# VectorE's order within a state of a selective scan: two scans, multiply-add, two scans, multiply-add

## The chip, the cores and the metric

The kernel runs on one core of a Trainium2 chip (trn2), as one program. The metric is the device time of one execution in microseconds (us). Engines are named as in the profile: PE is TensorE (matmuls), PEld its weight loads, DVE is VectorE, ACT is ScalarE, POOL is GpSimd, SP is SyncE, which issues most of the DMAs.

## The reference, cut to what matters

The input x has 8 sequences of 512 tokens with 256 channels. An adaptive layer norm is followed by a selective state-space layer (512 inner channels, 16 states) and, after a second adaptive layer norm, by a mixture of 8 experts with the best two chosen for each token. The change lies in the state-space layer:

```python
dt = softplus(dt @ W_dt + b_dt)
dA = exp(dt[..., None] * A)                      # A = -exp(A_log), 16 states
dBu = (dt * xc)[..., None] * Bm[:, :, None, :]
h[t] = dA[t] * h[t-1] + dBu[t]                   # along the 512 tokens
y = einsum('blds,bls->bld', h, Cm) + D_skip * xc
y = y * silu(z)
```

Everything is float32.

## The kernel before

The program has four stages one after the other, with barriers between them. Stage A does the state-space layer and the routing scores, stage B sorts tokens to experts, stage C runs the experts, stage D puts the results together. Only stage A is touched.

In stage A the inner channels lie on the partitions, in 4 chunks of 128 (index `c`), and the 512 tokens along the row. A sequence is one call of `body(n, p, has_o, has_p, has_r)` on every engine. It loops over the 16 states `s`. Besides the states of sequence n, a body carries parts of the input side of sequence n+1 (`has_p`), loads and the first norm of n+2 (`has_r`), and the output side of n-1 (`has_o`), each written by hand behind a certain state. Bodies 1 to 5 have all three, body 0 has no `has_o`, body 6 no `has_r`, body 7 only `has_o`. Each engine works its own list strictly in the order of the code and waits on semaphores.

For one state s, in the order in which the data go:

- POOL multiplies `dBu = u * B` for each chunk (L450), into a ring of 8 buffers.
- ACT computes `dA = exp(dt * a)` for each chunk (`decays`, L597), into a ring of only 2 PSUM banks: the one for a scan may start when the scan two before it has ended.
- DVE scans each chunk along the tokens (`scan`, L975) into `hs`, of which there are two (by parity of the state).
- PE transposes the four 128-token tiles of the four chunks (`states(n, s, i)`, L771) into PSUM: tiles 0 and 1 into bank T0, tiles 2 and 3 into bank T1, in the order 0, 2, then 1, 3. Tile 0 waits until all four scans of the state are done and the last multiply-add has read T0. Tile 1 waits until the first multiply-add has read T0.
- DVE multiplies tiles 0 and 1 by C and adds them to y (`add_y(n, p, s, i)`, L986, and L983 for state 0).
- ACT multiplies tiles 2 and 3 by C (`times_c(n, p, s, k)`, L583), and PE adds them up in PSUM by transposing matmuls (`add_up`, L780). At the start of a body PE transposes the finished y of the sequence before (`y_t`, L789, which waits for its last multiply-add).

DVE runs one state ahead with its scans: in its pass s it scans state s+1 and does the multiply-adds of state s. ACT's matching list is: decays 0 and 1 of state s+1, `times_c(s, 0)`, decay 2, in some passes an extra of the first kind, decay 3, `times_c(s, 1)`, in some passes an extra of the second kind, and again decay 0 of the next state. In DVE's passes (numbered by DVE's s; ACT's own index is one higher) the extras of the first kind are the first norm of n+2 (`p_norm`, L503, pass 4), both silus with their table loads (L543, L547, pass 6), `o_norm` (L503, pass 7), the squares of n+2 (L517, pass 8), `scores_in` (L612, pass 9), softplus parts (L568 to L571, passes 10 and 11, L575, pass 12) and one z copy (L539, passes 13 and 14). Those of the second kind are the copies into the convolution (`conv_in`, L534, passes 2 to 5, in the list of the sequence before their taps on DVE, L956, which run at the end of passes 2 to 5), `o_xhat` (L503, pass 9), softplus parts (passes 10 and 11), z copies (passes 12 and 13) and `norm` (L523, pass 14). DVE's own extras all stand at the end of its pass, behind the last scan and multiply-add: `o_skip` in pass 0 (PE's first `add_up` of the sequence waits for it), statistics, the taps, residuals, the choice of experts, and `dt` and `u` of the next sequence.

Of the kernel before, what the change touches and what calls it, by code (L numbers as in the profile page):

```python
# [107 lines left out]
def stage_a(nc, ctx, sem, ident, oh, wts, T, dA, Q, MOD_PS, YT, mod_d, b_d, h_d, xhat_d, base_d, slotx_d,  # L108
            x, norm_w, W_in, conv_w, conv_b, W_x, W_dt, b_dt, A_log, D_skip, W_out, Wg, cT, wmod):
    with ExitStack() as own:  # L110
# [138 lines left out]
        def after(eng, s, value):  # L249

            if not (isinstance(value, int) and value <= 0):
                eng.wait_ge(s, value)
# [638 lines left out]
        def _(dve):  # L891
# [53 lines left out]
            def p_stats(n):  # L945
                dve.wait_ge(s_pload, 32 * (n + 1))
                after(dve, s_ln1r, n)
                stats("p", n, xin, 0, s_ln1)

            def conv(n, p, c, bank):  # L950
                dve.wait_ge(s_xi, n * CH + c + 1)
                for k in range(PAD):
                    late = PAD - k
                    if k > 0:
                        dve.wait_ge(s_tap, (n * CH + c) * PAD + k)
                    nc.vector.scalar_tensor_tensor(xc[:, p, c, late:], Q[:, bank, 0:L - late], cw[:, c, k:k + 1], xc[:, p, c, late:],  # L956
                                                   ALU.mult, ALU.add).then_inc(s_tap, 1)
# [9 lines left out]
            def scan(n, s, c):  # L967
                i = s * CH + c
                if c == 0 and s >= 2:
                    dve.wait_ge(s_tr, n * UNITS + TI * (s - 1))  # L970
                elif c == 0:
                    after(dve, s_tr, (n - 1) * UNITS + TI * (NS - 1 + s))
                dve.wait_ge(s_dA, n * UNITS + i + 1)
                dve.wait_ge(s_dBu, n * UNITS + i + 1)
                nc.vector.tensor_tensor_scan(hs[:, s % 2, c, :], dA[:, i % DA_RING, :], dBu[:, i % RING, :], 0.0,  # L975
                                             ALU.mult, ALU.add).then_inc(s_scan, 1)

            def add_y(n, p, s, i):
                dve.wait_ge(s_tr, n * UNITS + TI * s + 2 * i + 1)
                c_s = ct[:, p, i, s:s + 1]  # L980
                if s == 0:
                    after(dve, s_yT, n)
                    ins = nc.vector.tensor_scalar(y[:, i, :], T[:, 0, :], c_s, None, ALU.mult)  # L983
                else:
                    dve.wait_ge(s_y, DT * (n * NS + s - 1) + i + 1)
                    ins = nc.vector.scalar_tensor_tensor(y[:, i, :], T[:, 0, :], c_s, y[:, i, :], ALU.mult, ALU.add)  # L986
                ins.then_inc(s_y, 1)

            def o_skip(n, p):
                dve.wait_ge(s_yT, n + 1)  # L990
                dve.wait_ge(s_acc, 2 * NS * (n + 1))
                for c in range(CH):
                    def by_tile(v):
                        return v.rearrange("p (i t) -> p i t", i=TI)
                    nc.vector.scalar_tensor_tensor(by_tile(gT[:, c, :]), by_tile(xc[:, p, c, :]), dsk[:, c:c + 1],
                                                   YT[:, :, c * P:(c + 1) * P], ALU.mult, ALU.add).then_inc(s_g, 1)

            def o_resid_half(n, half):
                dve.wait_ge(s_op, TI * n + 2 * half + 2)
                if half == 0:  # L1000
                    after(dve, s_bast, 16 * n)
                at = slice(2 * half, 2 * half + 2)
                nc.vector.tensor_tensor(x1[:, at, :], modo[:, 0, :].unsqueeze(1).to_broadcast([P, 2, D]),
                                        Q[:, OB, :].rearrange("p (i d) -> p i d", d=D), ALU.mult).then_inc(s_opr, 1)

            def o_resid(n):
                dve.wait_ge(s_opr, 2 * n + 2)
                link(nc.vector.tensor_tensor(x1[:, :, :], x1[:, :, :], xres[:, :, :], ALU.add), "o", n)
                stats("o", n, x1, 1, s_x1)

            def o_stats(n):
                dve.wait_ge(s_xfm, n + 1)
                stats("o", n, xf, 2, s_xf)

            def o_scores(n):
                dve.wait_ge(s_scp, n + 1)
                nc.vector.tensor_copy(sc[:, :, :], Q[:, XB, 0:TI * E].rearrange("p (i e) -> p i e", i=TI)).then_inc(s_scr, 1)

            def o_top(n):
                dve.wait_ge(s_scr, n + 1)  # L1020
                carrier()
                for i in range(TI):
                    last = nc.vector.max(top[:, i, :], sc[:, i, :])
                link(last, "o", n)
                carrier()
                for i in range(TI):
                    last = nc.vector.max_index(tix[:, i, :], top[:, i, :], sc[:, i, :])
                nc.vector.tensor_tensor(vd[:, 0, :], top[:, :, 1], top[:, :, 0], ALU.subtract).then_inc(s_vd, 1)
                link(last, "o", n)
                link(nc.vector.tensor_copy(tif[:, :, :], tix[:, :, 0:2]), "o", n)  # L1030
                for k in range(2):
                    nc.vector.tensor_tensor(oh[:, k, bass.ds(n * TI, TI), :], iota8[:, :].unsqueeze(1).to_broadcast([P, TI, E]),
                                            tif[:, :, k].unsqueeze(2).to_broadcast([P, TI, E]), ALU.is_equal)

            def o_base(n):
                dve.wait_ge(s_ve, n + 1)
                w1, w2 = wts[:, 0, bass.ds(n * TI, TI)], wts[:, 1, bass.ds(n * TI, TI)]
                link(nc.vector.tensor_scalar(vd[:, 2, :], vd[:, 1, :], 1.0, None, ALU.add), "o", n)
                link(nc.vector.reciprocal(vd[:, 2, :], vd[:, 2, :]), "o", n)
                link(nc.vector.tensor_tensor(vd[:, 1, :], vd[:, 1, :], vd[:, 2, :], ALU.mult), "o", n)  # L1040
                nc.vector.tensor_copy(w1, vd[:, 2, :])
                nc.vector.tensor_copy(w2, vd[:, 1, :])
                link(nc.vector.tensor_tensor(vd[:, 3, :], vd[:, 1, :], vd[:, 2, :], ALU.add), "o", n)

                dve.wait_ge(s_xh, n + 1)
                for i in range(TI):
                    last = nc.vector.scalar_tensor_tensor(xf[:, i, :], xf[:, i, :], vd[:, 3, i:i + 1], modo[:, 3, :],
                                                          ALU.mult, ALU.mult)
                last.then_inc(s_scaled, 1)
# [10 lines left out]
            def body(n, p, has_o, has_p, has_r):  # L1060
                if not has_o:
                    for c in range(CH):
                        scan(n, 0, c)

                def next_scan(s, c):
                    if s + 1 < NS:
                        scan(n, s + 1, c)
                    elif has_p:
                        scan(n + 1, 0, c)

                for s in range(NS):
                    next_scan(s, 0)
                    add_y(n, p, s, 0)
                    next_scan(s, 1)
                    next_scan(s, 2)
                    add_y(n, p, s, 1)
                    next_scan(s, 3)
                    if has_o and s == 0:
                        o_skip(n - 1, 1 - p)
                    if has_r and s == 1:  # L1080
                        p_stats(n + 2)
                    if has_p and s in (2, 3, 4, 5):
                        conv(n + 1, 1 - p, s - 2, XB)
                    if has_o and s == 3:
                        o_resid_half(n - 1, 0)
                    if has_o and s == 5:
                        o_resid_half(n - 1, 1)
                        o_resid(n - 1)
                    if has_o and s == 8:
                        o_stats(n - 1)  # L1090
                    if has_o and s == 9:
                        o_scores(n - 1)
                    if has_o and s == 10:
                        o_top(n - 1)
                    if has_o and s == 11:
                        o_base(n - 1)
                    if has_p and s == 12:
                        dt_sum(n + 1, 1 - p)
                    if has_p and s == 13:
                        dt_x(n + 1, 1 - p)  # L1100
                counted(P_LINKS * has_r, O_LINKS * has_o)

            def epilogue():
# [11 lines left out]
                o_base(NB - 1)  # L1115

            sequences(dve, prologue, body, epilogue)


# [451 lines left out]
```

## Time and profile before

| | |
|---|---|
| median of 3 runs | 1910.93 us (1910.68 to 1912.01) |
| profiled execution | 1918.14 us, its span 1916.3 us |
| DVE busy | 1327.5 us, 69% of the span |
| PE busy | 1321.5 us, 69% |
| POOL busy | 973.6 us, 51% |
| ACT busy | 893.6 us, 47% |
| stage A | scans from 91.4 us to 1160.7 us |
| stage C | about 1340 to 1890 us |

An idle time in brackets behind a row is the time for which the engine stood still before that instruction, and the arrow names the engine, the tile and the line that ended it. In a timeline, instructions of one kind that follow each other on an engine are merged into one row (x2 is two of them).

### The profile page before, as it was taken

The page shows a single profiled execution, that of the slowest core. Times are in us where ns is not written, and L with a number is a line of the kernel's source. Part 1 is how long each engine was busy: PE and PEld are TensorE (multiplying, and loading weights), DVE is VectorE, ACT ScalarE, POOL GpSimd, SP SyncE. Part 2 cuts the span into 40 slices and gives each one's busy share as a digit, 9 for nine tenths or more (in the row PEclk, how much of TensorE's full clock was granted, in tenths as well). Part 3 has the DMA queues.
Part 4 walks back from the last instruction along what each step waited for, and adds up shares of the span by engine and source line. Part 5 has one row for each costly group of instructions (what it writes and reads, how often), then busy time and mean ns, then how long its engine had stood idle before and what let it go on. Part 6 is the DMA issues. An engine that isn't in the chain of part 4 may idle for free. (4 is left out here: it accounts for less than half of the span.)

```text
span 1916.3 us, 27619 instructions
## 1 busy us (share of the span) xinstructions
PE 1321.5 (69%) x7744; PEld 1067.5 (56%) x7745; DVE 1327.5 (69%) x2543; ACT 893.6 (47%) x1299; POOL 973.6 (51%) x920
## 2 busy tenths in 40 slices
PE   2566767666667666767766655103999999999970
PEld 0244555454555544545544544103899999999960
DVE  1397988989889989989989994312454545545538
ACT  2568667667567667577567562001222222222200
POOL 2287868767767866867767781472111111111110
PEclk7788888989788989888989887556999999999995
DMA  4611111212112213112112110796211111111218
GB/s 162 239 53 56 34 39 50 89 36 88 46 40 74 65 34 105 39 34 87 40 35 78 36 50 26 205 249 195 64 39 36 36 38 33 38 36 35 71 63 292
DMA packets 97672, 146.78 MB, mean 77 GB/s; under 512 B 10457, under 2 KB 66265, under 8 KB 97441
## 3 DMA queue, kind: packets, MB, share of 16 engines
q1 hardware_dynamic: 78112, 109.59, 18.3%
q10 hardware_dynamic: 12928, 18.14, 3.4%
q0 software_dynamic: 6528, 17.87, 3.0%
q8 instruction: 41, 0.67, 0.1%
q14 instruction: 63, 0.51, 0.1%
HBM read 101.14 MB, written 44.42 MB: 76 GB/s over the span
## 5 line engine op out<-in xcount | busy, mean ns | idle before, releaser
L450 POOL TENSOR_TENSOR dBu<-u,brep 128x512 f32<-128x512 f32 x512 | 650.0, 1301 | 115.7 <-DVE hs L975 66.0
L975 DVE TENSOR_TENSOR_SCAN hs<-psum,dBu 128x512 f32<-128x512 f32 x512 | 608.7, 1209 | 68.3 <-ACT psum L597 58.9
L771 PE MATMUL psum<-ident,hs 128*128 128x128 f32 x2048 | 323.6, 309 | 205.8 <-DVE y L986 160.9
L597 ACT ACTIVATE psum<-dt,aneg 128x512 f32<-128x512 f32 x512 | 347.8, 688 | 231.0 <-DVE hs L975 227.4
L771 PEld LDWEIGHTS psum<-ident,hs 128*128 128x128 f32 x2048 | 261.7, 158 | 293.2 <-DVE y L986 211.7
L1355 ACT ACTIVATE w_now<-w_sb 128x2048 f32 x72 | 138.1, 1919 | 492.8 <-PE psum L1376 375.6
L1376 PE MATMUL psum<-xgT,w_now 128*128 128x128 f32 x2304 | 272.7, 277 | 0.0
L1376 PEld LDWEIGHTS psum<-xgT,w_now 128*128 128x128 f32 x2304 | 266.8, 194 | 0.1
L780 PE MATMUL psum<-ident,hc 128*128 128x128 f32 x1024 | 186.7, 315 | 113.5 <-ACT hc L583 74.6
L1387 PE MATMUL psum<-w_sb,hT 128*128 x1152 | 260.4, 379 | 0.0
L1432 DVE TENSOR_SCALAR hT<-psum,b_sb 128x128 f32<-128x128 f32 x576 | 155.5, 343 | 133.7 <-PE psum L1376 133.7
L1341 POOL TENSOR_TENSOR spare_c<-unfilled 128x1 f32<-128x1 f32 x72 | 13.3, 184 | 439.8 <-DVE ysb L1438 439.8
L583 ACT ACTIVATE hc<-psum,ct 128x512 f32<-128x512 f32 x256 | 174.2, 680 | 129.2 <-PE psum L771 128.5
L1387 PEld LDWEIGHTS psum<-w_sb,hT 128*128 128x128 f32 x1152 | 213.5, 190 | 26.1
L780 PEld LDWEIGHTS psum<-ident,hc 128*128 128x128 f32 x1024 | 140.4, 163 | 156.5 <-ACT hc L583 101.7
L986 DVE SCALAR_TENSOR_TENSOR y<-psum,ct,y 128x512 f32<-128x512 f32 x240 | 174.7, 728 | 34.1 <-PE psum L771 34.1
L1366 PE MATMUL psum<-ident,xg 128*128 128x128 f32 x144 | 28.1, 278 | 111.6 <-DMA xg<-slotx_d 110.3
L1438 DVE TENSOR_TENSOR ysb<-psum,b_sb 128x256 f32<-128x256 f32 x72 | 30.6, 425 | 92.4 <-PE psum L1387 92.4
L1366 PEld LDWEIGHTS psum<-ident,xg 128*128 128x128 f32 x144 | 20.2, 143 | 119.9 <-DMA xg<-slotx_d 111.4
L728 PE MATMUL psum<-xnT,win 128*128 128x512 f32 x128 | 66.1, 642 | 25.2 <-DVE xc L956 23.9
L956 DVE SCALAR_TENSOR_TENSOR xc<-psum,cw,xc 128x509 f32<-128x509 f32 (+2 forms) x96 | 71.2, 743 | 9.0 <-ACT xc L534 6.8
L1342 POOL DMA_INDIRECT y_d<-ysb,row_of_y x72 | 71.0, 986 | 11.5 <-POOL spare_c L1341 7.9
(150 smaller groups left out, 1351.1 us busy)
## 6 DMA issues: line engine op xcount, KB each, us to landing
brep<-b_d SPq DMA_DIRECT2D x128, 256.0 KB, 3.2
w_sb<-in_W ACTq DMA_DIRECT2D x12, 1024.0 KB
slotx_d<-dt SPq DMA_DIRECT2D x12, 771.0 KB, 11.3
xg<-slotx_d SPq DMA_DIRECT2D x72, 128.5 KB, 2.1
y<-y_d SPq DMA_DIRECT2D x8, 1024.0 KB, 8.3
xin<-in_x SPq DMA_DIRECT2D x8, 512.0 KB, 7.2
h_d<-hmod SPq DMA_DIRECT2D x8, 512.0 KB, 3.1
modo<-mod_d SPq DMA_DIRECT2D x8, 512.0 KB, 5.8
```

Source lines behind the costliest of these rows:

```text
L450: nc.gpsimd.tensor_tensor(dBu[:, i % RING, :], u[:, p, c, :], brep[:, s % 4, :], ALU.mult).then_inc(s_dBu, 1)
L583: nc.scalar.activation(hc[:, k, :], T[:, 1, :], ACT.Copy, scale=ct[:, p, DT + k, s:s + 1]).then_inc(s_hc, 1)
L597: nc.scalar.activation(dA[:, i % DA_RING, :], dt[:, p, c, :], ACT.Exp, scale=aneg[:, c, s:s + 1]).then_inc(s_dA, 1)
L771: last = nc.tensor.transpose(T[:, i // DT, c * P:(c + 1) * P], hs[:, s % 2, c, i * P:(i + 1) * P], ident[:, :])
L780: last = nc.tensor.matmul(YT[:, DT + k, c * P:(c + 1) * P], hc[:, k, c * P:(c + 1) * P], ident[:, :], start=(s == 0 and c == 0), stop=(s = ...
L956: nc.vector.scalar_tensor_tensor(xc[:, p, c, late:], Q[:, bank, 0:L - late], cw[:, c, k:k + 1], xc[:, p, c, late:], ALU.mult, ALU.add).the ...
L975: nc.vector.tensor_tensor_scan(hs[:, s % 2, c, :], dA[:, i % DA_RING, :], dBu[:, i % RING, :], 0.0, ALU.mult, ALU.add).then_inc(s_scan, 1)
L986: ins = nc.vector.scalar_tensor_tensor(y[:, i, :], T[:, 0, :], c_s, y[:, i, :], ALU.mult, ALU.add)
L1355: nc.scalar.activation(w1_now[:, r % 2, :, :], w1_sb[:, bass.ds(e * DC, DC), :], ACT.Copy).then_inc(s_w1, 1)
L1376: last = nc.tensor.matmul(H_PS[:, r % 2, f, :], w1_now[:, r % 2, k, f * P:(f + 1) * P], xgT[:, r % 2, k, :], start=(k == 0), stop=(k == DC ...
L1387: last = nc.tensor.matmul(Y_PS[:, r % 2, :], hT[:, r % 2, k, :], w2_sb[:, bass.ds(e * FC + k, 1), :].rearrange("p a d -> p (a d)"), start= ...
L1432: last = nc.vector.tensor_scalar(hT[:, r % 2, f, :], H_PS[:, r % 2, f, :], b1_sb[:, bass.ds(e * FC + f, 1)], 0.0, ALU.add, ALU.max)
```

## The change

Within each pass of the state loop, VectorE's first multiply-add stands behind the second scan and not the first, and the second multiply-add behind the fourth and not the third. Before: scan 0, add 0, scan 1, scan 2, add 1, scan 3. After: scan 0, scan 1, add 0, scan 2, scan 3, add 1. No instruction is added or removed, no wait's value is changed, and the lists of the other engines stay as they are.

```diff
                 for s in range(NS):
                     next_scan(s, 0)
+                    next_scan(s, 1)
                     add_y(n, p, s, 0)
-                    next_scan(s, 1)
                     next_scan(s, 2)
+                    next_scan(s, 3)
                     add_y(n, p, s, 1)
-                    next_scan(s, 3)
                     if has_o and s == 0:
                         o_skip(n - 1, 1 - p)
```

## Rows read from the trace of the kernel before

**Rows 1.** The page: busy time of each engine.

```profile
PE 1321.5 (69%) x7744; PEld 1067.5 (56%) x7745; DVE 1327.5 (69%) x2543; ACT 893.6 (47%) x1299; POOL 973.6 (51%) x920
```

**Rows 2.** Body 3: us, busy PE, PEld, DVE, ACT, POOL, clock, DMA share, GB/s.

```profile
507.00:645.00 138.00, 96.12 (x516) 70.56 (x516) 124.71 (x174) 92.76 (x153) 103.10 (x87) 0.87 0.19 60
```

**Rows 3.** Who waited for whom: total us, times, longest.

```profile
DVE hs L975 <- ACT psum L597: 58.9, 40, 6.9
...
DVE y L986 <- PE psum L771: 34.1, 29, 2.9
```

**Rows 4.** Timeline of DVE, pass 14 of body 3: start, duration.

```profile
626.57 1.21 DVE L975 TENSOR_TENSOR_SCAN hs<-psum,dBu 128x512 f32<-128x512 f32 x1
627.71 0.72 DVE L986 SCALAR_TENSOR_TENSOR y<-psum,ct,y 128x512 f32<-128x512 f32 x1
628.35 2.32 DVE L975 TENSOR_TENSOR_SCAN hs<-psum,dBu 128x512 f32<-128x512 f32 x2
630.59 0.72 DVE L986 SCALAR_TENSOR_TENSOR y<-psum,ct,y 128x512 f32<-128x512 f32 x1
...
633.10 1.22 DVE L975 TENSOR_TENSOR_SCAN hs<-psum,dBu 128x512 f32<-128x512 f32 x1 [0.66 <-ACT psum L597]
```

**Rows 5.** Timeline of ACT, the same pass.

```profile
629.59 0.69 ACT L597 ACTIVATE psum<-dt,aneg 128x512 f32<-128x512 f32 x1 [0.56 <-DVE hs L975]
630.22 0.67 ACT L583 ACTIVATE hc<-psum,ct 128x512 f32<-128x512 f32 x1
630.79 1.70 ACT L523 ACTIVATE xn<-hmod,rs 128x256 f32<-128x256 f32 x4
632.39 1.29 ACT L597 ACTIVATE psum<-dt,aneg 128x512 f32<-128x512 f32 x2
633.79 0.69 ACT L583 ACTIVATE hc<-psum,ct 128x512 f32<-128x512 f32 x1
```

**Rows 6.** Timeline of PE: passes 6, 14 and the next body's start.

```profile
557.11 1.97 PE L771 MATMUL psum<-ident,hs 128*128 128x128 f32 x8 [6.51 <-DVE y L986]
...
628.48 1.09 PE L771 MATMUL psum<-ident,hs 128*128 128x128 f32 x8 [2.79 <-DVE y L986]
...
632.57 1.09 PE L771 MATMUL psum<-ident,hs 128*128 128x128 f32 x8 [0.97 <-DVE hs L975]
...
637.97 1.04 PE L789 MATMUL psum<-ident,y 128*128 128x128 f32 x8
```

**Rows 7.** Timeline of ACT: the fourth decay of passes 4, 10, 11, 12, times_c of 9.

```profile
539.29 0.67 ACT L597 ACTIVATE psum<-dt,aneg 128x512 f32<-128x512 f32 x1
...
586.28 0.67 ACT L583 ACTIVATE hc<-psum,ct 128x512 f32<-128x512 f32 x1
...
594.08 0.69 ACT L597 ACTIVATE psum<-dt,aneg 128x512 f32<-128x512 f32 x1
...
604.26 0.68 ACT L597 ACTIVATE psum<-dt,aneg 128x512 f32<-128x512 f32 x1
...
614.00 0.68 ACT L597 ACTIVATE psum<-dt,aneg 128x512 f32<-128x512 f32 x1
```

**Rows 8.** Timeline of DVE, passes 1, 4, 6 and 10 to 12 of body 3.

```profile
512.12 0.75 DVE L986 SCALAR_TENSOR_TENSOR y<-psum,ct,y 128x512 f32<-128x512 f32 x1 [1.89 <-PE psum L771]
...
535.45 1.22 DVE L975 TENSOR_TENSOR_SCAN hs<-psum,dBu 128x512 f32<-128x512 f32 x1
...
564.20 2.41 DVE L975 TENSOR_TENSOR_SCAN hs<-psum,dBu 128x512 f32<-128x512 f32 x2 [4.26 <-ACT psum L597]
...
589.53 1.22 DVE L975 TENSOR_TENSOR_SCAN hs<-psum,dBu 128x512 f32<-128x512 f32 x1 [0.94 <-ACT psum L597]
...
594.93 1.21 DVE L975 TENSOR_TENSOR_SCAN hs<-psum,dBu 128x512 f32<-128x512 f32 x1
...
600.63 1.21 DVE L975 TENSOR_TENSOR_SCAN hs<-psum,dBu 128x512 f32<-128x512 f32 x1
...
610.31 1.22 DVE L975 TENSOR_TENSOR_SCAN hs<-psum,dBu 128x512 f32<-128x512 f32 x1
```

## The prediction

> **What bounds the kernel now.** The page comes first: over the whole span DVE is busy 69% and PE 69%, which says little, because the stages have different limits [rows 1]. The change is only in stage A, so I read that stage by stretches. In the 138 us of body 3 DVE is busy 124.7 us, POOL 103.1, PE 96.1 and ACT 92.8 [rows 2]: DVE is the engine that carries stage A, and a microsecond during which it stands still there is a microsecond of the kernel. The list of waits says who makes it stand: in its scans ACT's decays (58.9 us in 40 waits), in its multiply-adds PE's transposes (34.1 us in 29) [rows 3]. So the question is which of these waits the new order shortens, and which it makes.
>
> Next come the timelines of one quiet pass, engine by engine [rows 4 to 6]. On DVE a scan starts 1.12 to 1.14 us after the one or the multiply-add before it could, and a multiply-add takes 0.64 until the next may start (628.35 to 630.59 for two scans, 627.71 to 628.35 for an add) [rows 4]. A pass is thus 4 x 1.13 + 2 x 0.64 = 5.80 us in either order. That two scans next to each other cost no more than a scan and an add is in the same row, since the old order has such a pair too.
>
> **The change, edge by edge.** I count from the start of a pass. Old starts: scan 0 at 0, add 0 at 1.14, scan 1 at 1.78, scan 2 at 2.91, add 1 at 4.02, scan 3 at 4.66, end at 5.80. New: scan 1 at 1.13, add 0 at 2.26, scan 2 at 2.90, scan 3 at 4.03, add 1 at 5.16, end at 5.80. Three things move: add 0 is 1.12 later, scan 3 is 0.64 earlier, and the last thing in a pass is an add.
>
> First, what does not change. The dA ring has two banks, so a decay may start when the scan two before its own ends. In both orders one scan and one add lie between these two, for all four chunks. And PE may begin the next state's first transposes only when both scan 3 and add 1 are over, which comes at 5.88 in both.
>
> *a) Extra ACT work ahead of decay 3.* Where ACT does something long between decays 2 and 3, decay 3 comes late, at a time that the new order doesn't move: decay 2 waits for scan 0. Scan 3 now wants it at 4.03, where it was wanted at 4.66, and behind scan 3 the new order has still an add to do, 0.64 us that the old one had done already. The cost is (ready time minus 4.03), from 0 up to 0.64. Ready is the row's start plus its length plus 0.05 for the semaphore (632.39 + half of 1.29 to 633.10 is 0.06 [rows 4, 5]):
> - pass 4: 539.29 + 0.67 + 0.05 - 535.45 = 4.56, cost 0.53 [rows 7, 8]
> - pass 6, silus and table loads: DVE already stands 4.26 us, cost the full 0.64 [rows 8]
> - pass 10: 594.08 + 0.69 + 0.05 = 594.82, plus 1.13 + 0.64 is 596.59, against an old end of 594.93 + 1.13 = 596.06: cost 0.53 [rows 7, 8]
> - pass 11: 604.26 + 0.68 + 0.05 - 600.63 = 4.36, cost 0.33 [rows 7, 8]
> - pass 12: 614.00 + 0.68 + 0.05 - 610.31 = 4.42, cost 0.39 [rows 7, 8]
> The squares in pass 8 are shorter; they lie near the limit and I count them at nothing, with 0.64 as the upper bound.
>
> *b) Extra ACT work behind `times_c(s, 1)`.* That copy waits for PE's tiles 1 and 3, and these for add 0. PE started 0.77 after add 0 did (627.71 to 628.48 [rows 4, 6]), and the copy started 1.22 after PE (632.57 to 633.79 [rows 5, 6]). In the new order: 2.26 + 0.77 + 1.22 = 4.25. In the old one it started at 630.22 - 626.57 = 3.65, right behind decay 3 [rows 4, 5]. So it is 0.60 later, and everything behind it on ACT too. In a quiet pass decay 0 of the next state is then ready at about 4.25 + 0.57 + 0.74 = 5.56, ahead of 5.80: no cost. In pass 14 the `norm` lies between, and DVE stood still for it already (0.66): cost 0.60. Pass 9 is the same with `o_xhat` (0.94 of idle [rows 8], the copy at 586.28 [rows 7], 3.65 behind the pass's start as in pass 14): cost 0.60. In passes 2 to 5 the convolution's copy stands there, and DVE's taps need it at 5.80; it would be ready at about 4.25 + 0.57 + 0.7 + 0.05 = 5.57 (its length is an estimate from the other 128x512 copies in rows 5): no cost, but only 0.2 to spare. In passes 1, 11, 12 and 13 DVE has 2 us or more of its own extras behind, which hide 0.60.
>
> *c) The turn of the sequence.* PE's `y_t` waits for the last add of pass 15, which now ends the pass. Pass 15 starts at 633.10 [rows 4]; the add starts at +5.16, PE about 0.85 later, at 639.1, where it was 637.97 [rows 6]. Eight transposes further (0.93 in steady issue, an estimate from 1.09 less an overlap) `states(0, .)` starts at 640.03; +1.22 `times_c`, +0.57 decay 2, +0.74 ready: 642.56. Scan 2 of pass 0 wants it at 633.10 + 5.80 + 2.90 = 641.80. Cost 0.76, in bodies 1 to 7.
>
> *d) Waits that go.* In pass 1 add 0 stands 1.89 us for PE [rows 8]. The new order fills 1.13 of it with scan 1, whose decay is ready. But the next item is then scan 2, whose decay stands on ACT behind `times_c(s, 0)`, which waits for the same transposes. Old: add 0 at 512.12, scan 1, scan 2, add 1, scan 3. New: add 0 at 512.12, scan 2 where it was, scan 3, add 1. I take a gain of 0. It would be at most 1.13 where it occurs, in 7 bodies.
>
> The sum. A full body: c 0.76, pass 4 0.53, 6 0.64, 9 0.60, 10 0.53, 11 0.33, 12 0.39, 14 0.60 = 4.38, times 5 = 21.9. Body 0 (no output side: without c and pass 9): 3.02. Body 6 (no first norm of n+2: without passes 4 and 14): 3.25. Body 7 (c, pass 6, pass 9, and `o_norm` in pass 7, where nothing of a next sequence delays it, at 0.64): 2.64. Together 30.8 us. Stages B to D and POOL have no part: in the whole list of waits that rows 3 are from no scan waits for POOL, and the new order frees no `dBu` buffer later than the old. Against the profiled execution that is 1918.14 + 30.8 = 1948.9 (span 1916.3 + 30.8 = 1947.1); its 1918.14 lies 7.2 above the median of the runs, so against the median 1910.93 + 30.8 = 1941.7. I forecast 1942.
>
> Bounds. Below: delays can be swallowed by later waits of another cause (after pass 6, DVE stands for PE's matmuls in pass 7, and 0.2 of the 0.64 could vanish there). Half of the sum, 15, gives 1926. Above: pass 8 at 0.64 in 6 bodies, 3.8, and the next rival.
>
> **Rivals.**
>
> *Slower still, by PE's clock and the narrow passes.* After 2.79 us of idleness PE did its eight transposes in 1.09; after 6.51 in 1.97 [rows 6]. The new order stretches the gap ahead of tiles 1 and 3 by 1.12, to 3.9 in pass 14. If PE does those at the lower level, `times_c(s, 1)` is another 0.88 late: 6 x 0.88 = 5 us from pass 14 alone, the same from pass 9, and in passes 2 to 5 the 0.2 of reserve is gone, at 0.65 in up to 28 passes, 18 us. All of it gives 1942 + 28 = 1970, a third of it 1951. Against it: in passes 2 to 5 PE has projections in between and no long gap. The Trainium skill (TensorE: Matmul & The Clock Gate, Part 1) says the same of the gate, that idleness lowers the array's clock to 1.2 GHz; by that page alone the longer gaps of every pass would count against this change, while rows 6 show a gap of 2.79 that did not.
>
> *Faster: the adds stop waiting.* This is d) with the other outcome. PE gets 1.12 us more for tile 0 in every pass, and the waits of adds for PE are 34.1 us [rows 3]. Those of add 0 are about half. If scan 2's decay were not behind the same transposes, pass 1 would give 1.13 in 7 bodies and the smaller ones about as much again: 1911 - 16 = 1895. It decides from the point where decay 2 is ready before add 0 ends; rows 3 and 8 and ACT's order speak against it.
>
> *No change.* The delays of 0.3 to 0.6 are each smaller than ACT's idle time in the following pass, and if DVE's waits after them shrank by as much, the end would not move: 1911. For it speaks that ACT is busy only 92.8 of 138 us [rows 2]; against it that DVE, not ACT, carries the time, and has no idle time to give back outside passes 7 and 1.
>
> **How the numbers follow.** The forecast has 0.66, slower still (over 1950) 0.20, no change 0.07, faster 0.07. The range 1922 to 1964 leaves out the last two and the far end of the second, 0.07 + 0.07 + about 0.05, so holds 0.8. A measurement of this kernel tells about 0.2%, 4 us, from no change. Faster by more than that 0.07, within it 0.07, slower 0.86.
>
> **What would show it.** In the changed kernel's timeline of DVE, the second scan of a pair (scan 3) should have idle time for ACT in passes 4, 6, 10, 11 and 12, of 0.3 to 0.7 (4.3 in pass 6, where it was 4.26, with the add behind it), scan 0 about 1.3 behind pass 14 and 1.5 behind pass 9, and scan 2 of pass 0 about 0.8. The waits of scans for ACT should grow from 58.9 to about 80 to 90 us, more waits rather than longer ones; ACT's `times_c` should wait longer for PE. Stage C keeps its length. The prediction is wrong if scans 2 in pass 1 start earlier than in the old order, if the pass of two adjacent scans is not 5.80, or if PE's transposes slow down in many passes.

## The result and the profile after

The changed kernel takes 1953.98 us (median of 4 runs, 1951.75 to 1958.8), against 1911.47 us for the kernel before in the same comparison: a ratio of 1.0221, 95% interval 1.0195 to 1.0247. It is slower by 42.5 us. The time lies in the stated range, on the side that was expected, 12 us above the forecast of 1942. The profiled execution of it took 1951.75 us, its span 1950.0; the one of before was 7 us above its kernel's median, so between the two traces there are only 33.7 us. Stage A alone is a better measure: from the start of the first scan to that of the last it took 1068.0 us before and 1104.1 after, 36.1 more, and 1114.4 in a second trace of the changed kernel. What comes behind, where the order changes next to nothing, differs by up to 10 us between the traces of this case (756.9 us in the trace of before, 746.5 to 756.0 in those of the other kernels with the ring of two).

The page and the list of waits of the changed kernel, the rows that answer to [rows 1] and [rows 3]:

```profile
PE 1331.4 (68%) x7744; PEld 1090.0 (56%) x7745; DVE 1325.1 (68%) x2543; ACT 890.8 (46%) x1299; POOL 961.9 (49%) x920
```

```profile
ACT hc L583 <- PE psum L771: 265.1, 178, 6.5
...
DVE hs L975 <- ACT psum L597: 109.1, 89, 6.7
```

No engine has more work. DVE's scans waited for ACT's decays 40 times before and 89 times now, 50 us longer in all. The page gives the waits of the adds for PE as 11.5 us, where they were 34.1:

```profile
L986 DVE SCALAR_TENSOR_TENSOR y<-psum,ct,y 128x512 f32<-128x512 f32 x240 | 174.5, 727 | 11.5 <-PE psum L771 11.5
```

So the adds did stop waiting, as the "faster" rival said, and the time didn't fall: the scans behind them wait instead.

Where, pass by pass: the table gives the length of a DVE pass from one scan 0 to the next, mean over bodies 1 to 5, less that of before. It is worked out from the start times of the scans in the two traces, and in a second trace of the changed kernel from the experiments.

| pass | 0 | 1 | 2, 3 | 4 | 5 | 6 | 7 | 8 | 9 | 10 | 11 | 12 | 13 | 14 | 15 | sum |
|---|---|---|---|---|---|---|---|---|---|---|---|---|---|---|---|---|
| forecast | 0.76 | 0 | 0 | 0.53 | 0 | 0.64 | 0 | 0 | 0.60 | 0.53 | 0.33 | 0.39 | 0 | 0.60 | 0 | 4.38 |
| after | 1.26 | 0.07 | 0.01 | 0.50 | 0.00 | 0.57 | -0.67 | 0.19 | 0.69 | -0.59 | 0.12 | 0.99 | 0.01 | 0.44 | 0.57 | 4.2 |
| after, 2nd trace | 0.83 | 0.00 | 0.00 | 0.50 | 0.00 | 0.57 | 0.10 | 0.19 | 1.32 | 0.13 | 0.13 | 1.22 | 0.01 | 0.78 | 0.29 | 6.1 |

The rows of it, from the timeline of DVE in body 3 of the changed kernel (passes 4, 6, 11, 12, 15 and the next body's 0, twice):

```profile
551.97 1.22 DVE L975 TENSOR_TENSOR_SCAN hs<-psum,dBu 128x512 f32<-128x512 f32 x1 [0.45 <-ACT psum L597]
...
576.67 1.22 DVE L975 TENSOR_TENSOR_SCAN hs<-psum,dBu 128x512 f32<-128x512 f32 x1 [4.90 <-ACT psum L597]
...
617.59 1.22 DVE L975 TENSOR_TENSOR_SCAN hs<-psum,dBu 128x512 f32<-128x512 f32 x1 [0.25 <-ACT psum L597]
...
627.43 1.22 DVE L975 TENSOR_TENSOR_SCAN hs<-psum,dBu 128x512 f32<-128x512 f32 x1 [0.28 <-ACT psum L597]
629.22 3.42 DVE L961 TENSOR_TENSOR dt<-dt,u 128x2048 f32<-128x2048 f32 x1
...
647.58 2.34 DVE L975 TENSOR_TENSOR_SCAN hs<-psum,dBu 128x512 f32<-128x512 f32 x2 [1.19 <-ACT psum L597]
...
653.92 2.34 DVE L975 TENSOR_TENSOR_SCAN hs<-psum,dBu 128x512 f32<-128x512 f32 x2 [0.48 <-ACT psum L597]
...
658.43 2.34 DVE L975 TENSOR_TENSOR_SCAN hs<-psum,dBu 128x512 f32<-128x512 f32 x2 [1.13 <-ACT psum L597]
```

Passes 7, 9 and 10 differ by 0.6 to 0.8 between the two traces of one and the same kernel, pass 0 by 0.4, passes 14 and 15 by 0.3; the others are steadier, but for one body in pass 12. That the sum of the first trace, 4.2, is so near the forecast's 4.38 is in part luck: there pass 7 gave 0.67 back, for which the runs show no cause, and pass 10 0.59, and they made up for what passes 0, 12 and 15 cost above their terms. For whole bodies the two traces are longer than that of before by 4.8 and 4.9 us in body 0 (forecast 3.0), 20.8 and 30.3 in bodies 1 to 5 together (21.9), 3.3 and 4.3 in body 6 (3.3), and 7.8 and 7.4 in body 7 (2.6): 36.7 and 47.0 in all.

The reader is to see four things in the rows. Scan 3 of pass 4 waits 0.45, where it waited for nothing; scan 3 of pass 6 waits 4.90 where it was 4.26 [rows 8], which is the 0.64 of the add now behind it. Scan 0 behind pass 14 waits 1.19 and not 0.66 [rows 4]. Scan 0 of a quiet pass boundary (653.92) waits 0.48, which the forecast had at nothing. And the sum L961 takes 3.42, which no step of the forecast had.

The quiet boundary is explained on PE. Its timeline, passes 14 and 15 and the turn to the next body, the rows that answer to [rows 6]:

```profile
643.55 1.09 PE L771 MATMUL psum<-ident,hs 128*128 128x128 f32 x8 [1.88 <-DVE y L986]
...
650.61 1.97 PE L771 MATMUL psum<-ident,hs 128*128 128x128 f32 x8 [3.08 <-DVE y L986]
...
654.27 1.81 PE L789 MATMUL psum<-ident,y 128*128 128x128 f32 x8
```

Before the change the eight transposes of pass 15 in this body were these:

```profile
635.02 1.09 PE L771 MATMUL psum<-ident,hs 128*128 128x128 f32 x8 [1.35 <-DVE y L986]
```

In pass 14 the eight transposes of tiles 1 and 3 still take 1.09. In pass 15 they come behind 3.08 us of idleness (1.35 before the change) and take 1.97. The copy on ACT, decay 0 and scan 0 follow late, and `y_t`, 1.04 before, takes 1.81. The granted clock says what happened; it is the third number from the end, 1.00 and 0.50 of full speed in these two groups of the changed kernel (the columns are those of [rows 2]):

```profile
643.55:644.64 1.09, 1.09 (x10) 1.09 (x11) 1.09 (x2) 0.62 (x2) 1.09 (x2) 1.00 0.00 0
650.61:652.58 1.97, 1.97 (x9) 1.97 (x10) 1.97 (x2) 0.03 (x1) 1.97 (x3) 0.50 0.19 68
```

So 1.09 is eight transposes at 2.4 GHz, and 1.97 the same at 1.2 GHz. The other bodies bear it out. In the two traces of the changed kernel, pass 15 is 0.37 to 0.60 longer in the ten bodies in which these transposes took 1.79 or more, and in the four in which they took 1.09 or 1.10 it is unchanged three times and 0.46 longer once. The clock does it only together with the later add: in the kernel before they took 1.97 in bodies 0, 2 and 4 too, and pass 15 of bodies 0 and 4 was at its 5.80.

### The profile page after: what moved, and what is told of

The parts are those of the page before. It is cut to its first block and busy times, and to the rows that moved or that the text cites. A ratio compares the mean times of both kernels' runs of the same rounds, so it can differ in the third digit from the quotient of the medians.

```text
span 1950.0 us, 27619 instructions
## 1 busy us (share of the span) xinstructions
PE 1331.4 (68%) x7744; PEld 1090.0 (56%) x7745; DVE 1325.1 (68%) x2543; ACT 890.8 (46%) x1299; POOL 961.9 (49%) x920
## 5 line engine op out<-in xcount | busy, mean ns | idle before, releaser
L450 POOL TENSOR_TENSOR dBu<-u,brep 128x512 f32<-128x512 f32 x512 | 637.2, 1277 | 148.2 <-DVE hs L975 79.1
L975 DVE TENSOR_TENSOR_SCAN hs<-psum,dBu 128x512 f32<-128x512 f32 x512 | 601.1, 1208 | 124.2 <-ACT psum L597 109.1
L771 PE MATMUL psum<-ident,hs 128*128 128x128 f32 x2048 | 330.6, 314 | 279.3 <-DVE y L986 263.9
L771 PEld LDWEIGHTS psum<-ident,hs 128*128 128x128 f32 x2048 | 272.1, 162 | 357.8 <-DVE y L986 314.9
L597 ACT ACTIVATE psum<-dt,aneg 128x512 f32<-128x512 f32 x512 | 342.2, 688 | 128.7 <-DVE hs L975 121.4
L780 PE MATMUL psum<-ident,hc 128*128 128x128 f32 x1024 | 193.9, 326 | 78.6 <-ACT hc L583 40.5
L780 PEld LDWEIGHTS psum<-ident,hc 128*128 128x128 f32 x1024 | 146.4, 168 | 120.4 <-ACT hc L583 66.2
L986 DVE SCALAR_TENSOR_TENSOR y<-psum,ct,y 128x512 f32<-128x512 f32 x240 | 174.5, 727 | 11.5 <-PE psum L771 11.5
L1342 POOL DMA_INDIRECT y_d<-ysb,row_of_y x72 | 71.2, 988 | 11.5 <-POOL spare_c L1341 7.9
L1199 POOL DMA_INDIRECT slotx_d<-xs,slots x64 | 62.2, 971 | 29.4 <-issue 18.3
```

Source lines behind the costliest of these rows:

```text
L450: nc.gpsimd.tensor_tensor(dBu[:, i % RING, :], u[:, p, c, :], brep[:, s % 4, :], ALU.mult).then_inc(s_dBu, 1)
L597: nc.scalar.activation(dA[:, i % DA_RING, :], dt[:, p, c, :], ACT.Exp, scale=aneg[:, c, s:s + 1]).then_inc(s_dA, 1)
L771: last = nc.tensor.transpose(T[:, i // DT, c * P:(c + 1) * P], hs[:, s % 2, c, i * P:(i + 1) * P], ident[:, :])
L780: last = nc.tensor.matmul(YT[:, DT + k, c * P:(c + 1) * P], hc[:, k, c * P:(c + 1) * P], ident[:, :], start=(s == 0 and c == 0), stop=(s = ...
```

## The experiments

All times are medians of 4 to 6 runs, each with the ratio to the kernel before on the same chip.

**The change once more.**

> The changed kernel once more, as the measure for the others on this chip: 40 to 43 us over the kernel before (about 1953), as its runs so far.

1957.19 us, ratio 1.0231 (1.0208 to 1.0253), with the kernel before at 1909.99.

**One half of the change at a time.** The order of the first kernel:

```diff
                     next_scan(s, 0)
+                    next_scan(s, 1)
                     add_y(n, p, s, 0)
-                    next_scan(s, 1)
                     next_scan(s, 2)
                     add_y(n, p, s, 1)
                     next_scan(s, 3)
```

> Only the first multiply-add is moved: scan 0, scan 1, add 0, scan 2, add 1, scan 3. Ready-time theory (the copy behind add 0 is 0.60 late where ScalarE work follows it, nothing else): passes 9 and 14 alone pay, 0.60 x 13 = 8 us, 1919. Clock theory (the excess of about 11 us over the forecast is TensorE falling to its lower clock in pass 15, because its gap ahead of tiles 1 and 3 grew from 1.4 to 3.1 us, with a late start of the next sequence behind it): this kernel has that longer gap, so 8 + 11 = 19 us, 1930, and its eight transposes in pass 15 take 1.97 us instead of 1.09.

1932.51 us, ratio 1.0117 (1.0098 to 1.0136): 22.5 us, nearer to the clock theory's 19 than to 8. What it was to show came in part: the transposes of pass 15 took 1.74 to 1.97 in five of seven bodies, but 1.10 and 1.09 in bodies 0 and 3. The order of the second kernel:

```diff
                     next_scan(s, 2)
+                    next_scan(s, 3)
                     add_y(n, p, s, 1)
-                    next_scan(s, 3)
```

> Only the second multiply-add is moved: scan 0, add 0, scan 1, scan 2, scan 3, add 1. Ready-time theory: passes 4, 6, 10, 11, 12 pay (scan 3 wanted 0.64 earlier), and the turn of the sequence with 0.76: 23 us, 1934. Clock theory: add 0 is where it was, the gap is not longer, so nothing on top: the transposes in pass 15 stay at 1.09. If the two parts add up to the 42 of the whole, they don't interact; if this one alone gives 35 or more, the forecast's part a is mis-sized and not the clock.

1934.74 us, ratio 1.0124 (1.0105 to 1.0144): 24.8 us where 23 were forecast. Here too the sign named came only in part: pass 15 costs nothing in six of seven bodies, but its transposes did not stay at 1.09; they took 1.81 to 1.97 in four bodies, and with add 0 at its old place nothing waited for them. The two halves sum to 47.3, and the whole on the same chip is 1957.19 less 1909.99, 47.2: no interaction that these runs can tell. The passes, as above:

| pass | 0 | 4 | 6 | 7 | 8 | 9 | 10 | 11 | 12 | 14 | 15 |
|---|---|---|---|---|---|---|---|---|---|---|---|
| first half | 0.49 | 0.00 | 0.00 | -0.12 | 0.00 | 1.15 | -0.27 | 0.16 | -0.02 | 0.71 | 0.50 |
| second half | 0.16 | 0.50 | 0.57 | -0.12 | 0.19 | -0.01 | 0.00 | 0.12 | 1.22 | -0.23 | 0.19 |

The costs divide as parts a) and b) say: passes 4, 6, 8 and 12 belong to the scan that is wanted earlier, passes 9 and 14 to the add that comes later. The first half also has pass 15 and a pass 9 larger than its 0.60. The trace of the first half, body 3, PE and then DVE:

```profile
594.19 3.42 PE L816 MATMUL psum<-wg,gT 128*128 128x8 f32 x16
```

```profile
597.65 0.19 DVE L1017 COPY sc<-psum 128x32 f32<-128x32 f32 x1 [2.95 <-PE psum L816]
```

The router's 16 matmuls stand behind tiles 1 and 3 in PE's list. In the kernel before they took 1.85 in this body and DVE's copy of the scores did not wait; here they run at the lower clock (granted 0.50) and the copy waits 2.95 us. The length of pass 9 goes with this in all bodies: before the change and in the second half alone the 16 matmuls took 1.85 in bodies 1 to 7, and in the two traces of the whole change pass 9 is 0.51 or 0.52 longer in the nine bodies in which they took 1.85, and 1.38 to 1.74 in the five in which they took 2.15 to 3.42.

**Fillers on PE, pass 15.** The changed order, with this ahead of `states(n, s, 1)`:

```diff
+                    if has_p and s == NS - 1:
+                        pe.wait_ge(s_z, (n + 2) * CH)
+                        for k in range(20):
+                            nc.tensor.transpose(Q[:, XB, 0:P], ident[:, :], ident[:, :])
                     states(n, s, 1)
```

> The changed order, with 20 transposes of the identity (about 2.2 us, into a PSUM bank that is free there) ahead of tiles 1 and 3 in pass 15 of bodies 0 to 6, so that TensorE doesn't stand still for 3 us. Clock theory: its eight transposes behind take 1.09 instead of 1.97, the copy behind them is 0.9 earlier, the idle time of 0.5 before scan 0 of the next body goes, y_t is faster: 1.0 to 1.5 us a body, 7 to 10 us below the changed kernel (about 1944). Without the clock as cause: no change, or a few us slower if the filler itself delays the tiles.

1946.03 us, ratio 1.0195 (1.0175 to 1.0214): 11 us less than the changed kernel beside it by the medians, 7 by the ratios, with intervals that overlap. The trace is clearer for these passes. PE in pass 15 and at the turn:

```profile
648.36 2.35 PE L865 MATMUL psum<-ident 128*128 128x128 f32 x20
651.60 1.09 PE L771 MATMUL psum<-ident,hs 128*128 128x128 f32 x8 [0.89 <-DVE y L990]
...
654.49 1.09 PE L789 MATMUL psum<-ident,y 128*128 128x128 f32 x8 [0.36 <-DVE y L990]
```

With the gap filled the transposes take 1.09 again (granted clock 1.00), y_t too, scan 0 no longer waits, and passes 15 and 0 are 0.07 and 0.38 above those of before instead of 0.29 to 0.57 and 0.83 to 1.26. So what pass 15 cost was the clock behind the later add, and with its share of pass 0 it is about 1 us a body, 7 of the 42. That is a figure for these two passes: the sum over all passes of this trace, 5.2, lies between the 4.2 and 6.1 of the changed kernel, since pass 9 was 1.28 longer in it.

The same filler in the order with only the first half changed. From here on the loop stands in a helper: `keep_warm(bank, times)` transposes the identity so many times into the bank.

> Only the first multiply-add moved, with the 20 filler transposes in pass 15. The first swap alone cost 22.5 us where the ready times gave 8 and the clock 11. If the clock in pass 15 is what the first swap brings on top, the filler takes 7 to 11 us of it (about 1922). If the rest is elsewhere (pass 9, where the trace of the first swap shows 1.15 us more than before), less.

1939.36 us, ratio 1.0145 (1.0128 to 1.0163): no gain, rather a loss beside the first half's 1.0117. Its trace has passes 15 and 0 back at 0.02 and -0.13, but pass 9 at 1.45, pass 7 at 0.46 and pass 10 at 0.40. What was gained in one place was lost in others; in pass 9 the router's matmuls took 3.42 instead of 1.85 in all of bodies 1 to 6. Fillers in pass 9 and just ahead of it:

```diff
+                    if has_o and s == 8:
+                        pe.wait_ge(s_opr, 2 * n)
+                        keep_warm(Q[:, OB, 0:P], 18)
                     states(n, s, 1)
```

(and 6 ahead of `xf_t` in pass 9.)

> Only the first multiply-add moved, with fillers on TensorE in pass 8 (18 transposes ahead of tiles 1 and 3) and pass 9 (6 ahead of the transposes of xf), in bodies 1 to 7. The trace of the first swap alone shows the clock at its lower level in pass 9 of some bodies: the router's 16 matmuls take 3.42 us instead of 1.85 and VectorE's copy of the scores waits 2.95 us. Theory (the part of the first swap beyond the 8 us of ready times is TensorE's clock, and it sits in pass 9 rather than in 15): pass 9 is 0.5 above the kernel before in every body instead of 1.15 on average, the router takes 1.85, and the whole is 5 to 8 us below the first swap alone (about 1926). Rival (something else makes pass 9 long): the router is fast and the pass stays above 8 us in some bodies.

1932.97 us, ratio 1.0129 (1.0104 to 1.0153): not 5 to 8 us less, so the time alone decides nothing. The trace: PE, then DVE, pass 9 of body 3.

```profile
592.51 1.85 PE L816 MATMUL psum<-wg,gT 128*128 128x8 f32 x16
```

```profile
594.40 0.19 DVE L1025 COPY sc<-psum 128x32 f32<-128x32 f32 x1 [0.41 <-PE psum L816]
```

Pass 9 is 0.5 above before in bodies 1 to 4 (7.39 against 6.88 in body 3), where the first half alone had up to 8.99, and 0.69 in the mean instead of 1.15. It was expected in every body, and was not so in all: in bodies 5 and 6 the router's matmuls still took 2.27 and 3.42, and pass 9 was 1.38 and 1.57 longer. The mechanism is there in that pass; its saving, 2 us over bodies 1 to 5, is below what the runs can tell.

**Where y_t stands.** In the changed order, `y_t` behind the first tiles:

```diff
-                if has_o:
-                    pe.wait_ge(s_z, (n + 1) * CH)
-                    y_t(n - 1)
                 for s in range(NS):
                     states(n, s, 0)
                     states(n, s, 2)
+                    if has_o and s == 0:
+                        pe.wait_ge(s_z, (n + 1) * CH)
+                        y_t(n - 1)
```

> The changed order with TensorE's transpose of the finished y behind the first tiles of the next sequence and not ahead of them. Theory of part c (y_t now starts with the end of pass 15 and pushes tiles 0 and 2, the copy, decay 2 and scan 2 of pass 0): that is 0.76 to 1.13 us a body in bodies 1 to 7, so 5 to 8 us below the changed kernel. If it gains nothing, the wait of scan 2 in pass 0 has another cause.

1955.1 us, ratio 1.0222 (1.0202 to 1.0241): no gain that can be measured, a miss. Its trace says why; DVE at the start of body 4:

```profile
656.69 2.34 DVE L975 TENSOR_TENSOR_SCAN hs<-psum,dBu 128x512 f32<-128x512 f32 x2 [0.48 <-ACT psum L597]
659.84 0.75 DVE L983 TENSOR_SCALAR y<-psum,ct 128x512 f32<-128x512 f32 x1 [0.82 <-PE psum L789]
660.51 2.33 DVE L975 TENSOR_TENSOR_SCAN hs<-psum,dBu 128x512 f32<-128x512 f32 x2
```

Scan 2 no longer waits, but add 0 does, for `y_t` itself: state 0's add overwrites the y that `y_t` reads. The edit moved the wait and did not take it away. Pass 0 is 0.55 above before in the mean, but 0.94 to 1.06 in bodies 2, 4 and 5. So this run doesn't price part c). What does is how long `y_t` took in the two traces of the changed kernel, in the bodies whose `y_t` was at 1.04 to 1.06 before: where it took 1.81 to 1.91, pass 0 is 1.65 to 1.78 longer (three bodies), and where it took 1.04 to 1.12, 0.43 to 0.96, 0.72 in the mean (seven bodies).

**Pass 12 in the old order,** all others in the new:

```diff
                     next_scan(s, 0)
-                    next_scan(s, 1)
+                    if s != 12:
+                        next_scan(s, 1)
                     add_y(n, p, s, 0)
+                    if s == 12:
+                        next_scan(s, 1)
...
```

> The changed order, but pass 12 keeps the old one. In pass 12 the traces show the sum into dt (L961) at 3.41 us instead of 2.57, besides the 0.4 of the late decay. Theory (VectorE and GpSimd exclude each other where VectorE reads two SBUF operands, and the new order starts the sum just behind the start of a GpSimd multiplication and not near its end): 1.2 us in each of 7 bodies come back, 8 us, about 1946, and L961 is 2.57 again. Rival (the length of L961 is moved by something earlier, since all passes ahead keep the new order): it stays at 3.4 and only 0.4 x 7 = 3 us come back.

1945.03 us, ratio 1.0174 (1.0161 to 1.0188), against 1.0221 and 1.0231 for the whole change: 9 to 11 us come back, where 8 were forecast, and pass 12 is exactly as before (0.00), as the theory had it. The length of L961, least, median and greatest ns; first in the kernel before, then the changed one, then this one:

```profile
L961 DVE TENSOR_TENSOR dt<-dt,u x8: 2268/2568/2577, 79.9 to 1027.4; 128x2048 f32<-128x2048 f32 x8
```

```profile
L961 DVE TENSOR_TENSOR dt<-dt,u x8: 2281/3412/3436, 78.5 to 1053.5; 128x2048 f32<-128x2048 f32 x8
```

```profile
L961 DVE TENSOR_TENSOR dt<-dt,u x8: 2265/2564/2586, 80.9 to 1056.1; 128x2048 f32<-128x2048 f32 x8
```

POOL's four `dBu` multiplications beside it, from the timelines of before and after:

```profile
612.78 7.02 POOL L450 TENSOR_TENSOR dBu<-u,brep 128x512 f32<-128x512 f32 x4
```

```profile
625.51 4.97 POOL L450 TENSOR_TENSOR dBu<-u,brep 128x512 f32<-128x512 f32 x4
```

After, the sum starts at 629.22, about when POOL's last of four does (625.51 + 3 x 1.24 = 629.23), and ends at 632.64; POOL ends at 630.48, and from there to the end are 2.16 us, near the 2.27 to 2.29 that L961 takes where no multiplication runs when it starts. In body 5 of the same trace the sum started as a POOL multiplication ended too, but went first: it took 2.28, POOL's four took 7.11, and pass 12 was only 0.09 longer. Before, it starts at 616.10, near the end of POOL's third (612.78 + 3 x 1.24 = 616.50), and POOL's four take 2 us longer. Each waits for the other's instruction to end. The Trainium skill (SBUF — State Buffer, SBUF: two separate sides) says this: VectorE with two SBUF inputs and GpSimd hold a shared pair of ports for a whole instruction, whoever comes first. The trace agrees, with the 2.16 us behind POOL's end and the 2 us that POOL's four are longer where the sum came first.

**The decays in a ring of four in SBUF,** in the old order and in the new:

```diff
-DA_RING = 2
+DA_RING = 4
...
+        dA = sb("dA", [P, DA_RING, L])
```

> The old order with the decays in a ring of four in SBUF instead of two PSUM banks. Theory (ScalarE's decays come late because the two banks tie them to the scan two before): the decay that stands ahead of the silus in pass 6 no longer waits 5 us for scan 0, so the 4.26 us of idle time there goes, with most of the other waits of scans for ScalarE: 30 to 45 us faster than before, 1866 to 1880. Rival: VectorE then reads two operands from SBUF while GpSimd does too, and both get slower; each 1% on the scans is 6 us.

> The same ring of four with the new order. If the loss of the new order comes from decay 3 standing close to its due time because of the ring of two, the deeper ring takes most of it: the distance to ring4_old falls from 42 to 5 to 20 us. What is left is what doesn't hang on the ring: the copy behind add 0 (8 us), the turn of the sequence, TensorE's clock. If the distance stays at 35 or more, the ring has no part in it.

2179.3 us, ratio 1.1402 (1.1381 to 1.1423), and 2204.79, ratio 1.1537 (1.1508 to 1.1566). The rival won by far. The page of the old order with this ring:

```profile
L451 POOL TENSOR_TENSOR dBu<-u,brep 128x512 f32<-128x512 f32 x512 | 975.2, 1938 | 53.8 <-DVE u L966 53.8
L976 DVE TENSOR_TENSOR_SCAN hs<-dA,dBu 128x512 f32<-128x512 f32 x512 | 910.4, 1803 | 28.9 <-ACT dA L598 28.3
```

Scans take 1803 ns instead of 1209 and POOL's multiplications 1938 instead of 1301. The waits for ACT did halve (58.9 to 28.3 us), and the orders are 25 us apart instead of 42 to 47, but with every scan 50% longer this is another kernel; it doesn't tell how much of the order's price hangs on the ring of two.

**Fillers in the long gaps, in both orders:** 30 transposes in pass 0 ahead of the first `add_up` (which waits for the skip), 40 and 36 in pass 6 (while ACT does the silus), and in the new order those of pass 15.

```diff
+                    if has_p and s == 6:
+                        pe.wait_ge(s_tap, (n + 2) * CH * PAD)
+                        keep_warm(Q[:, XB, 0:P], 40)
                     states(n, s, 1)
                     states(n, s, 3)
+                    if has_o and s == 0:
+                        pe.wait_ge(s_hc, 2 * n * NS + 2)
+                        keep_warm(T[:, 1, 0:P], 30)
                     add_up(n, s, 0)
...
+                    if has_p and s == 6:
+                        keep_warm(Q[:, XB, 0:P], 36)
                     add_up(n, s, 1)
```

> The old order, with filler transposes of the identity in TensorE's long gaps of pass 0 (30, while it waits for the skip) and pass 6 (40 and 36, while ScalarE does the silus) so that it comes out of them at the higher clock. Clock theory: the add of pass 1 that stands 1.9 us for TensorE, the 4.3 us x_proj in pass 7 and the 2 us wait behind it shrink: 1 to 1.5 us in pass 1 and 1 to 2 us in pass 7 of each body, 15 to 25 us faster than before, 1888 to 1897. Rival: these passes hang on ScalarE or the fillers last too long: no gain or a loss.

> The changed order with the same fillers and that of pass 15. Against fill_old this is the price of the order with TensorE kept warm in the worst gaps: the ready-time terms alone are 31 us by the forecast; with the 6 us of L961 about 35. If it is still 42 or more above fill_old, the clock had no part in the order's price; if it falls to 20, the clock had more than I thought.

The old order with fillers takes 1896.02 us, ratio 0.9921 (0.9906 to 0.9935): 15.5 us faster than the kernel before, at the edge of what was expected, and better than both. Its timeline of DVE, pass 1 of body 3, and of PE, pass 7:

```profile
506.02 0.75 DVE L998 SCALAR_TENSOR_TENSOR y<-psum,ct,y 128x512 f32<-128x512 f32 x1 [1.36 <-PE psum L771]
506.68 2.33 DVE L987 TENSOR_TENSOR_SCAN hs<-psum,dBu 128x512 f32<-128x512 f32 x2
```

```profile
560.01 3.60 PE L745 MATMUL psum<-xc,wx 128*96 128x512 f32 x8
563.45 1.04 PE L771 MATMUL psum<-ident,hs 128*128 128x128 f32 x8
```

In the kernel before, that x_proj of pass 7 took longer:

```profile
567.43 4.28 PE L745 MATMUL psum<-xc,wx 128*96 128x512 f32 x8
```

Pass 1 is 1.45 shorter and pass 7 by 0.65; all others are as before to within 0.14. The passes of all bodies sum to 15.0 us less. The new order with fillers takes 1934.92, ratio 1.0119 (1.0104 to 1.0134): 39 us above the old with the same fillers, where the forecast's own terms and L961 make 35. This 39 is not the price of the order with the clock taken out: in the new order with fillers the router's matmuls still took 3.42 in six of bodies 1 to 7, where the old had 1.85 in all, and pass 9 was 1.68 longer. So the clock still has a part in the 39, and a price without it was not measured.

## Why the prediction was right, and what was mis-sized

*Which engine bounds, and which waits decide: right.* DVE's work did not change (1327.5 and 1325.1 us busy), and what grew are scans waiting for ACT, 58.9 to 109.1 us (114.6 in the second trace); that is above the 80 to 90 that the forecast named as its sign, and more waits rather than longer ones, as it said.

*Part a), scan 3 wanted earlier: right in mechanism, nearly right in size.* Passes 4, 6 and 11 were put at 0.53, 0.64 and 0.33 and came as 0.50, 0.57 and 0.12; pass 8, counted at nothing, is 0.19. The second half alone, put at 23 us, cost 24.8. Pass 10 was put at 0.53; it was -0.59 and 0.13 in two traces and 0.00 in the second half alone. Scan 3 does wait (0.94 us at 607.72 in body 3), and DVE came to its extras behind the last scan and add 6.84 us into the pass instead of 6.54 in body 3, and 6.85 instead of 5.81 in bodies 2 and 4. The traces show what took it back: these extras took 3.74 us in body 3 instead of 4.56. Among them is a tiny DVE instruction with two SBUF operands (L1028, 128x4). It takes 0.15 us in the epilogue, where no POOL multiplication runs; beside one it ended 0.02 to 0.03 us behind the end of POOL's instruction in six of seven bodies before and in all seven after, and so it took 1.08 in body 3 before and 0.28 after. It is the meeting of pass 12 again, here with a gain.

*Part a), pass 12: the largest hidden cost.* Put at 0.39, it was 0.99 to 1.22: 0.4 for the decay, 0.85 for the sum that now meets POOL. The experiment gave 9 to 11 us back. The forecast said that POOL has no part and read it only as a supplier of `dBu`; that it can hold up a DVE instruction was in the trace of before, in the length of L961 and in POOL's four beside it.

*Part b), the copy behind add 0: right in size, where PE's clock is full.* Pass 14 came as 0.44 and 0.78 for 0.60. Pass 9 came as 0.69 and 1.32: 0.52 where the router's matmuls took 1.85, and 1.4 to 1.7 where PE ran at the lower clock. Scan 0 behind pass 9 waits 0.95 us in body 3, where the forecast had 1.5; 0.42 of the wait stands before DVE's copy of the scores instead.

*Part c), the turn: right in size, where PE's clock is full.* 0.76 was forecast, 0.83 and 1.26 measured: 0.72 in the mean of the seven bodies whose `y_t` ran at full clock, 1.65 to 1.78 in the three where it did not. The one edit that moved `y_t` moved the wait only.

*Part d), no gain from waits that go: right.* In pass 1, add 0 waits 0.77 in the changed kernel instead of 1.89, and scan 2 behind it 1.39 for its decay; the pass is longer by 0.00 to 0.07. DVE in body 3:

```profile
524.09 0.75 DVE L986 SCALAR_TENSOR_TENSOR y<-psum,ct,y 128x512 f32<-128x512 f32 x1 [0.77 <-PE psum L771]
526.22 2.34 DVE L975 TENSOR_TENSOR_SCAN hs<-psum,dBu 128x512 f32<-128x512 f32 x2 [1.39 <-ACT psum L597]
```

*The clock: named as a rival at 0.20, counted at nothing in the sum, and it was there.* The median came out beyond 1950, the point at which that rival was to be read. But not where it was put: passes 2 to 5 kept their length in bodies 1 to 6, pass 14 stayed near its 0.60, and passes 15, 0 and 9 and body 7 paid. The argument against this rival rested on one body. [rows 6] show eight transposes in 1.09 behind a gap of 2.79 in pass 14 of body 3; in the same trace those of pass 14 took 1.97 in bodies 2 and 4 behind the same 2.79, and were below full clock in six of the eight bodies. Nor did the gap of pass 14 grow to 3.9: after the change it was 1.88 in body 3 and 3.42 at most, and the transposes took 1.09 in all bodies but one. So pass 14 did not pay for the clock, but not for the reason given. Of the 128 groups of eight for tiles 1 and 3, 33 were below full clock before (over 1.3 us) and 39 and 35 after: not many more, but in places that count.

Body 7 has no projections to keep PE busy. It was put at 2.6 us and cost 7.8 and 7.4 in the two traces, 6.2 in the first half alone and 1.7 in the second. Most of the excess, 5.9 and 5.8 us, lies in passes 2, 3 and 5, which the forecast had at nothing. Pass 2 of it, PE, in the changed kernel:

```profile
1096.88 1.97 PE L771 MATMUL psum<-ident,hs 128*128 128x128 f32 x8 [1.74 <-DVE y L986]
1098.64 1.06 PE L780 MATMUL psum<-ident,hc 128*128 128x128 f32 x4
1099.50 1.06 PE L800 MATMUL psum<-hres,ident 128*128 128x256 f32 x2
1100.35 3.20 PE L802 MATMUL psum<-wout,gT 128*128 128x256 f32 x8
```

The same pass in the kernel before:

```profile
1067.90 1.09 PE L771 MATMUL psum<-ident,hs 128*128 128x128 f32 x8 [0.67 <-DVE y L986]
...
1069.70 1.89 PE L802 MATMUL psum<-wout,gT 128*128 128x256 f32 x8
```

The transposes took 1.09 behind 0.67 of idleness, and the output projection 1.89 instead of 3.20. No run filled PE's gaps in passes 2 to 5 of body 7, so the clock as the cause there is read from these rows and not shown by an edit. The cost varies: in the four other traces of the order with a filler or one detail changed, body 7 was 3.2 to 5.1 us longer.

The step that fell short is thus the sum's zero for the clock, with pass 12's 0.39 beside it. Of the 12 us between forecast and median, about 5 to 6 are L961 and 5 are body 7; pass 15 and the larger passes 0 and 9 come on top, and pass 10 and the smaller pass 11 are to be taken off. How much of the clock's part each execution pays varies (36.7 and 47.0 us in all in the two traces), so this account is one of sizes and not exact, and that the median lies only 12 us above the forecast owes something to terms that erred to both sides.

## What to carry to other kernels

On an engine that works in order, moving an instruction later is not free even if nothing is added and every wait is shorter there: follow what waits behind it on the other engines, and when that is due back. Here waits of 0.1 to 0.7 us in about half of the 16 passes of each of 8 sequences, with the clock and L961 on top, made 42 us. Before counting a gap on TensorE as free, look at what the next group costs at the lower clock, and in all repetitions of the place, not in one; and of every VectorE instruction with two SBUF operands ask what GpSimd is doing at that time, since a shift of 1 us can cost or save nearly a whole GpSimd instruction.

## What the runs showed of the hardware that was not expected

- A scan with both operands in SBUF, beside POOL's multiplications, took 1803 ns, and with one of them in PSUM 1209; POOL's went from 1301 to 1938.
- A 128x2048 sum with two SBUF operands took 2.27 us alone and 2.57 or 3.42 by when it met POOL, and a 128x4 one 0.15 alone and up to 1.31. The wait stands in the profile as length of the instruction, not as idle time before it.
- TensorE ran eight transposes in 1.97 us behind a gap of 1.74 us in one place and in 1.09 behind 1.88 or 2.79 in others, and behind the same gap of 2.79 in 1.09 in one body and 1.97 in two others: the gap just ahead does not decide alone. The Trainium skill (TensorE: Matmul & The Clock Gate, Part 1) ties the level to recent activity rather than to one gap, with which these rows agree.
- 76 and 30 otherwise useless transposes per sequence made the kernel 15.5 us faster.
